# Low-rank time-step rows of a fused GNN, Mamba and mixture-of-experts kernel: plain fp32 in place of a split into reduced-precision parts

## The chip, the cores and the metric

The kernel runs on one core of one Trainium2 chip. The metric is device time in microseconds (us) of one launch; before the change the median of three runs is 1839.88 us (1839.81 to 1846.79).

## The reference, cut to what matters

`N` is 8192 rows of 128 features. A graph layer multiplies by a dense adjacency matrix of 8192 x 8192; its result goes through a Mamba block, and that through a layer with 8 experts.

```python
h = relu(adj @ layernorm(x) @ gcn_w + gcn_b); h = layernorm(h) * ln_g + ln_b
xz = h @ w_in;  xc, z = xz[:, :256], xz[:, 256:]
u = silu(conv4(xc) + conv_b)
dbc = u @ w_xp                                  # 8 + 16 + 16 columns
dt = softplus(dbc[:, :8] @ w_dt + b_dt)         # the eight low-rank rows of the time step
B, C = dbc[:, 8:24], dbc[:, 24:40]
# scan over the rows, 256 channels x 16 states: hst = exp(dt*A)*hst + dt*B*u;  y = hst @ C
x = x + ((y + u * D_skip) * silu(z)) @ w_out
H = gelu(layernorm(x) @ W1 + b1); probs = softmax(H @ Wg + bg)
out = x + probs[e] * (H @ Wd[e] + bd[e])        # e = argmax of probs, 512 hidden, 8 experts
```

The change touches `dbc[:, :8] @ w_dt` alone.

## The kernel before, in words

The 8192 rows are cut into 16 tiles of 512 (`T`). Tensors lie transposed, channels on the partitions and the 512 rows of a tile along the free axis. The kernel is a software pipeline written out by hand. Body `i` has five stages, each on another tile: `adjacency` for tile i+2, `front` (graph layer, projection, convolution, time step) for tile i+1, `mamba` (the scan) for tile i, `ffn` for tile i-1 and `experts` for tile i-2. A body has 16 slots (`SLOTS`), one for each Mamba state; slot `s` of each stage is written beside slot `s` of the others. Bodies 4 to 13 lie in a hardware loop of two bodies a round, the rest is unrolled. No scheduler orders anything: each engine runs its own instructions in the order written, and waits on semaphores.

What the engines do in a slot of a full body:

- VectorE (DVE): two scans (L609), the sums of the expert outputs that were read from PSUM (`combine`, L590 to L598), `y_sum` plus the last slot's `h_c` (L661), and `inject` for the next slot (L725).
- GpSimd (POOL): `h_c` = `hidden` times C (L355), which waits until `inject` of the next slot is done and so runs beside the scans. In four slots it also subtracts to form the low part of `H` (L346).
- TensorE (PE): four adjacency products of 128x512 (L781), and in every second slot one unit of twelve expert products into `ps_e` (`unit`); DVE's `combine(v)` reads unit v // 2.
- ScalarE (ACT): copies of the scan's last column (L406), the decays (L413), activations and copies out of PSUM.
- SyncE (SP): the DMAs, in order: adjacency blocks, each behind the matmuls that free its ring buffer (`adj_used`), and between them the broadcast rows of B and C (`bc_ring`), which go through DRAM (`bc_dram`).

The time step is made in slots 8 to 13 of `front`. In slot 8 PE multiplies `u_sb` by `w_xp`. The host has laid out `w_xp` so that the product holds B and C on partitions 96 to 127 and the same eight low-rank rows three times, from partitions 0, 32 and 64. In slot 9 ACT copies B and C (L495), casts partitions 0 to 71 to the reduced type fp32r into `low_parts` (L497), and copies the third set once more, uncast, into `low_raw` (L498). POOL then replaces rows 64 to 71 of `low_parts` by `low_raw` minus their cast (L339), after its `h_c` of slot 8 and ahead of that of slot 9. The weights `wdt_parts` hold, on partitions 0, 32 and 64, the cast, what the cast lost, and the cast, formed once at the start (ACT L388, DVE L565). One product of 72 partitions thus adds up high x high, high x rest and rest x high. PE makes it for the first 128 channels in slot 9 (it waits for `low_split`, POOL's semaphore) and for the other 128 in slot 10. DVE reads both in slot 11 (L632) and 13 (L637). Every product of the kernel that is in fp32r appears in the trace as one matmul, every plain fp32 product of 512 columns as two.

Behind the product of slot 10 PE has 16 gate products of 8 columns (for `logit`), six adjacency products, and unit 6, which DVE's `combine(12)` reads in slot 13. PE also waits for DVE: in slot 3 for `x1` (L622), in slot 14 for `coef_parts` (L712).

Of the kernel before, what the change touches and what calls it, by code (L numbers as in the profile page):

```python
# [5 lines left out]
P = 128  # L6
T = 512
SLOTS = 16
# [8 lines left out]
ALU = mybir.AluOpType  # L17
ACT = mybir.ActivationFunctionType
F32 = mybir.dt.float32
# [15 lines left out]
def gnn_mamba_moe(nc, x_rows, x_cols, adj, vecs, consts, sel, gcn_w, w_in, w_xp, w_dt, w_out, W1, Wg, Wd, bd, out):  # L35
# [10 lines left out]
    with ExitStack() as ctx:  # L46
# [19 lines left out]
        wdt_parts = sb("wdt_parts", [72, 2, P], F32R)  # L66
# [20 lines left out]
        low_parts = sb("low_parts", [96, T], F32R)  # L87
        coef_t = low_parts[:, 0:P]

        rows_sb = sb("rows_sb", [72, T])  # L90
        bc_rows, low_raw = rows_sb[0:2 * SLOTS, :], rows_sb[64:72, :]
# [31 lines left out]
        wdt_sb = x1[0:72, 0:2 * P].rearrange("p (h c) -> p h c", h=2)  # L123
# [69 lines left out]
        low_split = sem("low_split")  # L193
# [76 lines left out]
        def _(sp):  # L270
# [6 lines left out]
            def small_weights():  # L277
                for dst, src in ((vec_sb, vecs), (const_sb, consts), (gcn_sb, gcn_w), (win_sb, w_in),
                                 (wxp_sb, w_xp), (wdt_sb, w_dt), (wout_sb, w_out), (w1_sb, W1), (wg_sb, Wg),
                                 (bd_sb, bd)):  # L280
                    sp.dma_start(dst if isinstance(dst, bass.AP) else dst[:], src).then_inc(weights_in, 16)
# [46 lines left out]
        def _(pool):  # L328
            def body(i, p, adjacency, front, mamba, ffn, experts):
                c = Count(pool, i)  # L330
                q = 1 - p
                for s in range(SLOTS):

                    if front and s == 9:

                        if mamba:
                            c.wait(hc_ready, 0, s)
                        c.wait(low_ready, 1, 1)
                        nc.gpsimd.tensor_tensor(low_parts[64:72], low_raw, low_parts[64:72].bitcast(F32),  # L339
                                                ALU.subtract).then_inc(low_split, 1)  # L340
                        c.wait(low_split, 1, 1)
# [19 lines left out]
        def _(act):  # L361
# [26 lines left out]
            nc.scalar.copy(wdt_parts[:], wdt_sb)  # L388
# [8 lines left out]
            def body(i, p, adjacency, front, mamba, ffn, experts):  # L397
# [19 lines left out]
                for s in range(SLOTS):  # L417
# [73 lines left out]
                    if front and s == 9:  # L491

                        c.wait(dbc_done, 1, 1)
                        c.wait(rows_out, 1, 0)
                        nc.scalar.copy(bc_rows, ps_f[96:128, 0]).then_inc(rows_ready, 1)  # L495
                        c.wait(dt_done, 1, 0)
                        nc.scalar.copy(low_parts[0:72], ps_f[0:72, 0])  # L497
                        nc.scalar.copy(low_raw, ps_f[64:72, 0]).then_inc(low_ready, 1)  # L498
# [32 lines left out]
        def _(dve):  # L531
# [10 lines left out]
            for e in range(10):  # L542
# [11 lines left out]
                if e >= 2:  # L554
# [10 lines left out]
            nc.vector.tensor_tensor(wdt_parts[32:40], wdt_sb[32:40], wdt_parts[32:40].bitcast(F32), ALU.subtract  # L565
                                    ).then_inc(start_v, 1)
# [6 lines left out]
            dve.wait_ge(start_v, 9)  # L573
# [157 lines left out]
        def _(pe):  # L731
# [12 lines left out]
            def body(i, p, adjacency, front, mamba, ffn, experts):  # L744
                c = Count(pe, i)
                q = 1 - p
                for s in range(SLOTS):
# [37 lines left out]
                    if front and s == 0:  # L785
                        if isinstance(i, int) and i == -1:
                            pe.wait_ge(start_a, 3)
                            pe.wait_ge(start_v, 9)
                        c.wait(agg_ready, 1, 1)
                        c.wait(dt_ready, 1, 0)  # L790
                        product(ps_f[:, 0], [(gcn_sb[:], front_a[:])]).then_inc(gcn_done, 1)
# [35 lines left out]
                    if front and s == 9:  # L827
                        c.wait(low_split, 1, 1)
                        if ffn:
                            c.wait(h_ready, -1, 2)  # L830
                        product(ps_f[:, 1], [(wdt_parts[:, 0], low_parts[0:72])]).then_inc(dt_done, 1)
# [3 lines left out]
                    if front and s == 10:  # L835
                        c.wait(rows_ready, 1, 1)
                        product(ps_f[:, 0], [(wdt_parts[:, 1], low_parts[0:72])]).then_inc(dt_done, 1)
# [84 lines left out]
```

## Time and profile before

| | |
|---|---|
| median of three runs | 1839.88 us |
| the profiled execution | 1840.22 us |
| its span, from the first to the last instruction | 1838.1 us |
| PE busy | 1648.3 us (90%) |
| VectorE busy | 1663.1 us (90%) |
| ScalarE busy | 829.9 us (45%) |
| GpSimd busy | 708.7 us (39%) |
| POOL L339, the subtraction of the low rows | 16 of 1480 ns, 23.7 us |
| ACT L497, L498, the cast and the raw copy | 16 of 583 ns and 16 of 578 ns |
| PE products of `low_parts` with `wdt_parts` | 32, 642 ns in the record |

The 1.5 to 2 us between span and execution lie outside the instructions. A matmul's recorded duration contains its way through the array and overlaps the next one; what it costs the engine is the distance between starts. Idle time is shown in square brackets in a timeline, with what ended it. Two engines are about equally busy on average, so where the time goes has to be read from who waits for whom, stretch by stretch.

### The profile page before, as it was taken

The numbers are of one execution on the slowest core, as the hardware profiler recorded it, in microseconds if no ns is written. First come the engines' busy times: TensorE is split into PE (matmuls) and PEld (weight loads), VectorE is DVE, ScalarE is ACT, GpSimd is POOL, SyncE is SP. The second block draws the span as 40 slices with busy tenths as digits, with TensorE's granted clock in tenths as the row PEclk, the third lists the DMA queues.
The fourth block names the chain that finished last, engine by engine and source line by source line (L and its number), as shares of the span: only waits on it lengthen the run. The fifth ranks groups of instructions, "written<-read, shape, count | busy, mean of one in ns | idle before, by whom it ended". The sixth has DMA issues, their size and how long they took to land. (4 is left out here: it accounts for less than half of the span.)

```text
span 1838.1 us, 18846 instructions
## 1 busy us (share of the span) xinstructions
PE 1648.3 (90%) x4856; PEld 896.8 (49%) x4856; DVE 1663.1 (90%) x2089; ACT 829.9 (45%) x1457; POOL 708.7 (39%) x340
## 2 busy tenths in 40 slices
PE   5999697999999999999999999999999999764668
PEld 2444243555554555455554545455555555432447
DVE  8118999999999999999989999999999999999974
ACT  3034455463636354463625454363635446362522
POOL 0003444434444344434434444444434443444431
PEclk9999898999999999999999999999999999876779
DMA  9889786766677777667676776667776676322210
GB/s 334 289 258 354 279 292 251 252 238 254 240 271 248 258 246 250 231 219 280 236 258 223 266 252 238 233 221 284 247 250 241 241 256 229 116 88 86 100 33 12
DMA packets 124749, 420.56 MB, mean 229 GB/s; under 512 B 13404, under 2 KB 22180, under 8 KB 124420
## 3 DMA queue, kind: packets, MB, share of 16 engines
q1 hardware_dynamic: 123236, 413.51, 64.1%
q10 hardware_dynamic: 1440, 6.29, 0.9%
q14 instruction: 54, 0.44, 0.1%
q8 instruction: 19, 0.31, 0.1%
HBM read 414.51 MB, written 5.24 MB: 228 GB/s over the span
## 5 line engine op out<-in xcount | busy, mean ns | idle before, releaser
L781 PE MATMUL ps_adj<-ring,nodes 128*128 128x512 f32 x2048 | 962.9, 611 | 31.4 <-DVE nodes L557 17.4
L355 POOL TENSOR_TENSOR h_c<-hidden,bc_ring 128x1024 f32<-128x1024 f32 x256 | 605.0, 2363 | 946.4 <-DVE inject L725 865.4
L609 DVE TENSOR_TENSOR_SCAN hidden<-decay,state,inject 128x512 f32<-128x512 f32 x512 | 627.6, 1268 | 37.2 <-POOL h_c L355 9.3
L781 PEld LDWEIGHTS ps_adj<-ring,nodes 128*128 128x128 f32 x2048 | 397.7, 196 | 490.9 <-issue 449.0
L734 PE MATMUL ps_e<-wd_parts,H_parts 128*128 128x512 f32 x1536 | 437.6, 436 | 9.8 <-DVE odd_acc L593 5.3
L734 PEld LDWEIGHTS ps_e<-wd_parts,H_parts 128*128 128x128 f32 x1536 | 299.5, 196 | 129.2 <-issue 52.5
L413 ACT ACTIVATE decay<-dt_sb,negA 128x512 f32<-128x512 f32 x512 | 340.1, 713 | 1.3 <-DVE dt_sb L637 1.0
L725 DVE TENSOR_TENSOR inject<-dtu_sb,bc_ring 128x1024 f32<-128x1024 f32 x256 | 318.2, 1243 | 15.4 <-DMA bc_ring<-bc_dram 13.2
L661 DVE TENSOR_TENSOR y_sum<-y_sum,h_c 128x1024 f32<-128x1024 f32 x224 | 301.2, 1345 | 0.5 <-POOL h_c L355 0.4
L406 ACT COPY state<-hidden 128x2 f32<-128x2 f32 x256 | 49.4, 193 | 515.5 <-DVE hidden L609 515.1
L593 DVE SCALAR_TENSOR_TENSOR out_sb<-ps_e,coef,out_sb 128x128 f32<-128x128 f32 x256 | 84.7, 331 | 31.1 <-PE ps_e L734 28.8
L346 POOL TENSOR_TENSOR H_parts<-H,H_parts 128x512 fp32r<-128x512 f32 x64 | 82.3, 1286 | 38.5 <-ACT H_parts L518 38.5
L674 DVE SCALAR_TENSOR_TENSOR u_sb<-conv_in,vec_sb,u_sb 128x512 f32<-128x512 f32 x96 | 65.0, 746 | 11.3 <-ACT u_sb L466 11.3
L339 POOL TENSOR_TENSOR low_parts<-rows_sb,low_parts 8x512 fp32r<-8x512 f32 x16 | 23.7, 1480 | 125.1 <-ACT rows_sb L498 123.4
L734 PEld LDWEIGHTS ps_y<-wg_sb,H 128*128 128x128 f32 x512 | 65.5, 207 | 9.8 <-ACT H L525 6.0
L734 PE MATMUL ps_y<-wg_sb,H 128*128 128x8 f32 x512 | 64.1, 265 | 5.5 <-ACT H L525 5.5
L593 DVE SCALAR_TENSOR_TENSOR odd_acc<-ps_e,coef,odd_acc 128x128 f32<-128x128 f32 x192 | 65.7, 342 | 0.0
L734 PE MATMUL ps_y<-x,const_sb 128*128 128x512 f32 x32 | 21.5, 759 | 46.2 <-DVE x L622 46.2
L734 PE MATMUL ps_f<-front_a,win_sb 128*128 128x512 f32 x128 | 60.3, 594 | 1.3 <-ACT conv_in L459 1.2
L625 DVE TENSOR_TENSOR front_a<-ps_f,front_b 128x512 f32<-128x512 f32 x16 | 10.8, 677 | 42.8 <-ACT front_b L440 42.8
L734 PE MATMUL ps_f<-soft,w_sb 128*128 128x512 f32 x64 | 33.8, 655 | 15.0 <-DVE soft L665 15.0
L734 PE MATMUL ps_f<-u_sb,wxp_sb 128*128 128x512 f32 x64 | 35.5, 683 | 13.0 <-ACT H L487 8.3
(108 smaller groups left out, 1100.7 us busy)
## 6 DMA issues: line engine op xcount, KB each, us to landing
ring<-adj SPq DMA_DIRECT2D x512, 512.0 KB, 4.2
bc_ring<-bc_dram SPq DMA_DIRECT2D x256, 512.0 KB, 4.8
nodes<-x_rows ACTq DMA_DIRECT2D x8, 512.0 KB, 12.4
x_tile<-x_cols SPq DMA_DIRECT2D x16, 256.0 KB, 5.7
out<-out_sb SPq DMA_DIRECT2D x16, 256.0 KB, 4.0
decay<-Wd ACTq DMA_DIRECT2D x1, 1024.0 KB
dt_sb<-Wd ACTq DMA_DIRECT2D x1, 1024.0 KB
bc_dram<-rows_sb SPq DMA_DIRECT2D x16, 64.0 KB
```

The lines of the kernel that those rows point to most:

```text
L339: nc.gpsimd.tensor_tensor(low_parts[64:72], low_raw, low_parts[64:72].bitcast(F32), ALU.subtract).then_inc(low_split, 1)
L346: nc.gpsimd.tensor_tensor(H_parts[:, 1, place], H[:, :, b * P:(b + 1) * P], H_parts[:, 0, place].bitcast(F32), ALU.subtract).then_inc(lo_s ...
L355: nc.gpsimd.tensor_tensor(h_c[:, s % 2], hidden[:, s % 2], over_halves(bc_ring[:, s % BC_RING, 1]), ALU.mult).then_inc(hc_ready, 1)
L406: nc.scalar.copy(state[:, :, t:t + 1], hidden[:, t % 2, :, T - 1:T]).then_inc(state_ready, 1)
L413: exp = nc.scalar.activation(decay[:, t % 2, h], dt_sb[:, p if d == 0 else q, h], ACT.Exp, scale=negA[:, h, t:t + 1])
L593: step = nc.vector.scalar_tensor_tensor(out=acc, in0=src, scalar=w, in1=acc, op0=ALU.mult, op1=ALU.add)
L609: scan = nc.vector.tensor_tensor_scan(hidden[:, s % 2, h], decay[:, s % 2, h], inject[:, h], state[:, h, s:s + 1], ALU.mult, ALU.add)
L661: nc.vector.tensor_tensor(y_sum[:], y_sum[:], h_c[:, (s - 1) % 2], ALU.add).then_inc(y_step, 1)
L674: nc.vector.scalar_tensor_tensor(out=u_sb[:, h], in0=conv_in[:, h, k:k + T], scalar=vec("conv_w", TAPS * h + k), in1=u_sb[:, h], op0=ALU.m ...
L725: nc.vector.tensor_tensor(inject[:], dtu_sb[:], over_halves(bc_ring[:, t % BC_RING, 0]), ALU.mult).then_inc(inject_ready, 1)
L734: last = nc.tensor.matmul(dst, stationary, moving, start=(n == 0), stop=(n == len(pairs) - 1))
L781: last = nc.tensor.matmul(ps_adj[:, 0], nodes[:, m], ring[:, g % RING, m % GROUP], start=(m == 0), stop=(m == J - 1))
```

## The change

The eight rows are copied once out of PSUM as plain fp32 (`low_sb`), and the weights are the eight rows as loaded. The cast, the raw copy, POOL's subtraction with its semaphore, and the two set-up instructions for the weights go. Both products are plain fp32 over 8 partitions. Buffers that shared memory with these (`coef_t`, `bc_rows`) get their own.

```diff
-        wdt_parts = sb("wdt_parts", [72, 2, P], F32R)
+        wdt_sb = sb("wdt_sb", [8, 2, P])
...
-                    if front and s == 9:
-
-                        if mamba:
-                            c.wait(hc_ready, 0, s)
-                        c.wait(low_ready, 1, 1)
-                        nc.gpsimd.tensor_tensor(low_parts[64:72], low_raw, low_parts[64:72].bitcast(F32),
-                                                ALU.subtract).then_inc(low_split, 1)
-                        c.wait(low_split, 1, 1)
...
-            nc.scalar.copy(wdt_parts[:], wdt_sb)
...
                         c.wait(dt_done, 1, 0)
-                        nc.scalar.copy(low_parts[0:72], ps_f[0:72, 0])
-                        nc.scalar.copy(low_raw, ps_f[64:72, 0]).then_inc(low_ready, 1)
+                        nc.scalar.copy(low_sb[:], ps_f[0:8, 0]).then_inc(low_ready, 1)
...
-            nc.vector.tensor_tensor(wdt_parts[32:40], wdt_sb[32:40], wdt_parts[32:40].bitcast(F32), ALU.subtract
-                                    ).then_inc(start_v, 1)
...
                     if front and s == 9:
-                        c.wait(low_split, 1, 1)
+                        c.wait(low_ready, 1, 1)
                         if ffn:
                             c.wait(h_ready, -1, 2)
-                        product(ps_f[:, 1], [(wdt_parts[:, 0], low_parts[0:72])]).then_inc(dt_done, 1)
+                        product(ps_f[:, 1], [(wdt_sb[:, 0], low_sb[:])]).then_inc(dt_done, 1)
...
                     if front and s == 10:
                         c.wait(rows_ready, 1, 1)
-                        product(ps_f[:, 0], [(wdt_parts[:, 1], low_parts[0:72])]).then_inc(dt_done, 1)
+                        product(ps_f[:, 0], [(wdt_sb[:, 1], low_sb[:])]).then_inc(dt_done, 1)
```

PE's instructions in slots 9 and 10 of a full body, before (`soft` holds the normalized input of the expert layer, `w_sb` is W1, `[waits ...]` names the semaphores):

```order
L734 MATMUL ps_f<-low_parts,wdt_parts 128x512 [waits h_ready,low_split]
L734 MATMUL ps_y<-soft,w_sb 128x512 [waits h_ready]
L781 MATMUL ps_adj<-ring,nodes 128x512 [waits ring_in0]
L781 MATMUL ps_adj<-ring,nodes 128x512
L734 MATMUL ps_e<-wd_parts,H_parts 128x512 [waits acc_step]
L734 MATMUL ps_e<-wd_parts,H_parts 128x512 x11
L781 MATMUL ps_adj<-ring,nodes 128x512 [waits ring_in1]
L781 MATMUL ps_adj<-ring,nodes 128x512
L734 MATMUL ps_f<-low_parts,wdt_parts 128x512 [waits rows_ready]
```

The same place after the change:

```order
L719 MATMUL ps_f<-low_sb,wdt_sb 128x512 [waits h_ready,low_ready]
L719 MATMUL ps_y<-soft,w_sb 128x512 [waits h_ready]
L766 MATMUL ps_adj<-ring,nodes 128x512 [waits ring_in0]
L766 MATMUL ps_adj<-ring,nodes 128x512
L719 MATMUL ps_e<-wd_parts,H_parts 128x512 [waits acc_step]
L719 MATMUL ps_e<-wd_parts,H_parts 128x512 x11
L766 MATMUL ps_adj<-ring,nodes 128x512 [waits ring_in1]
L766 MATMUL ps_adj<-ring,nodes 128x512
L719 MATMUL ps_f<-low_sb,wdt_sb 128x512 [waits rows_ready]
```

Nothing has moved; the first product waits for ACT's semaphore where it waited for POOL's, and the operands are others.

POOL's instructions around slot 9, before (the first `h_c` is that of slot 8):

```order
L355 TENSOR_TENSOR h_c<-hidden,bc_ring 128x1024 [waits y_step,inject_ready]
L224 REGISTER_ALU [waits hc_ready]
L339 TENSOR_TENSOR low_parts<-rows_sb,low_parts 8x512 [waits low_ready]
L224 REGISTER_ALU [waits scan_ready,low_split]
L355 TENSOR_TENSOR h_c<-hidden,bc_ring 128x1024 [waits y_step,inject_ready]
```

The same place after the change:

```order
L344 TENSOR_TENSOR h_c<-hidden,bc_ring 128x1024 [waits y_step,inject_ready]
L221 REGISTER_ALU [waits scan_ready]
L344 TENSOR_TENSOR h_c<-hidden,bc_ring 128x1024 [waits y_step,inject_ready]
L221 REGISTER_ALU [waits scan_ready]
L344 TENSOR_TENSOR h_c<-hidden,bc_ring 128x1024 [waits y_step,inject_ready]
```

POOL goes from one `h_c` to the next, and its wait for its own subtraction is gone too.

## Rows read from the trace of the kernel before

**Rows 1.** Busy time by engine in the last stretch (start:end, length, busy)

```profile
1771.00:1838.00 67.00, 60.88 (x251) 46.45 (x251) 30.63 (x90) 14.34 (x21) 9.41 (x8) 0.93 0.04 12
```

**Rows 2.** Waits of DVE, 400 to 1600 us: waiter, awaited: total us, times, longest

```profile
DVE hidden L609 <- POOL h_c L355: 9.3, 3, 3.3
...
DVE out_sb L593 <- PE ps_e L734: 1.2, 1, 1.2
```

**Rows 3.** Waits of PE, 400 to 1600 us

```profile
PE ps_y L734 <- DVE x L622: 29.1, 9, 8.9
...
PE ps_f L734 <- POOL low_parts L339: 10.5, 10, 1.4
```

**Rows 4.** Timeline of slot 9 in one full body: start, length, what

```profile
901.05 3.60 PE L781 MATMUL ps_adj<-ring,nodes 128*128 128x512 f32 x8
...
902.52 0.58 ACT L498 COPY rows_sb<-ps_f 8x512 f32<-8x512 f32 x1
...
904.35 1.26 POOL L339 TENSOR_TENSOR low_parts<-rows_sb,low_parts 8x512 fp32r<-8x512 f32 x1 [0.16 <-DVE hidden L609]
...
904.71 1.98 DVE L661 TENSOR_TENSOR y_sum<-y_sum,h_c 128x1024 f32<-128x1024 f32 x1
...
905.74 0.49 PE L734 MATMUL ps_f<-low_parts,wdt_parts 72*128 72x512 f32 x1 [1.09 <-POOL low_parts L339]
...
906.07 1.02 PE L734 MATMUL ps_y<-soft,w_sb 128*128 128x512 f32 x2
```

**Rows 5.** All of L661 and of L725: ns minimum/median/maximum

```profile
L661 DVE TENSOR_TENSOR y_sum<-y_sum,h_c x224: 1207/1217/2295, 157.4 to 1771.4; 128x1024 f32<-128x1024 f32 x112
...
L725 DVE TENSOR_TENSOR inject<-dtu_sb,bc_ring x256: 1218/1226/2301, 144.6 to 1765.2; 128x1024 f32<-128x1024 f32 x128
```

**Rows 6.** Slot 9 of two other bodies, timeline of DVE and PE

```profile
801.33 2.27 DVE L661 TENSOR_TENSOR y_sum<-y_sum,h_c 128x1024 f32<-128x1024 f32 x1
...
802.65 0.49 PE L734 MATMUL ps_f<-low_parts,wdt_parts 72*128 72x512 f32 x1
...
1636.51 1.94 DVE L661 TENSOR_TENSOR y_sum<-y_sum,h_c 128x1024 f32<-128x1024 f32 x1
```

**Rows 7.** Timeline of PE around the second product, slot 10

```profile
911.45 1.88 PE L781 MATMUL ps_adj<-ring,nodes 128*128 128x512 f32 x4
...
912.76 0.79 PE L734 MATMUL ps_f<-low_parts,wdt_parts 72*128 72x512 f32 x1
...
913.40 4.72 PE L734 MATMUL ps_y<-wg_sb,H 128*128 128x8 f32 x32
```

**Rows 8.** Unit 6 on PE and its first reader on DVE, in four bodies

```profile
822.01 3.36 PE L734 MATMUL ps_e<-wd_parts,H_parts 128*128 128x512 f32 x12
...
825.50 0.35 DVE L593 SCALAR_TENSOR_TENSOR out_sb<-ps_e,coef,out_sb 128x128 f32<-128x128 f32 x1
...
925.06 3.35 PE L734 MATMUL ps_e<-wd_parts,H_parts 128*128 128x512 f32 x12
...
928.54 0.35 DVE L593 SCALAR_TENSOR_TENSOR out_sb<-ps_e,coef,out_sb 128x128 f32<-128x128 f32 x1
...
1031.69 3.36 PE L734 MATMUL ps_e<-wd_parts,H_parts 128*128 128x512 f32 x12
...
1035.61 0.33 DVE L593 SCALAR_TENSOR_TENSOR out_sb<-ps_e,coef,out_sb 128x128 f32<-128x128 f32 x1
...
1245.71 0.35 DVE L593 SCALAR_TENSOR_TENSOR out_sb<-ps_e,coef,out_sb 128x128 f32<-128x128 f32 x1 [1.16 <-PE ps_e L734]
```

**Rows 9.** Timeline of PE, SP and DVE at the start of the first scan

```profile
126.58 15.61 PE L781 MATMUL ps_adj<-ring,nodes 128*128 128x512 f32 x36
...
137.45 0.42 SPq L309 DMA_DIRECT2D bc_ring<-bc_dram  x1
...
144.59 1.23 DVE L725 TENSOR_TENSOR inject<-dtu_sb,bc_ring 128x1024 f32<-128x1024 f32 x1 [13.18 <-DMA bc_ring<-bc_dram]
```

**Rows 10.** Busy by stretch; the third figure from the end is TensorE's granted clock

```profile
915.00:920.00 5.00, 5.00 (x22) 3.97 (x22) 4.91 (x8) 3.29 (x7) 0.71 (x2) 0.57 0.46 185
```

More of the change, by code:

```diff
@@ L85, in gnn_mamba_moe @@
         dtu_sb = sb("dtu_sb", [P, 2, T])
[L87 to L91, printed above, removed]
+        coef_t = sb("coef_t", [96, P], F32R)[:]
+        low_sb = sb("low_sb", [8, T])
+        bc_rows = sb("bc_rows", [2 * SLOTS, T])[:]
         bc_ring = sb("bc_ring", [P, BC_RING, 2, T])
@@ L122, in gnn_mamba_moe @@
         bd_sb = soft[0:96, 1].rearrange("p (b c) -> p b c", b=BLOCKS)
-        wdt_sb = x1[0:72, 0:2 * P].rearrange("p (h c) -> p h c", h=2)
         row_sum, row_rstd = odd_acc[:, 0:J], odd_acc[:, J:2 * J]
@@ L192, in gnn_mamba_moe @@
         base_done, base_ready = sem("base_done"), sem("base_ready")
-        low_split = sem("low_split")
         hi_split, lo_split = sem("hi_split", BLOCKS), sem("lo_split", BLOCKS)
@@ L278, in small_weights @@
                 for dst, src in ((vec_sb, vecs), (const_sb, consts), (gcn_sb, gcn_w), (win_sb, w_in),
-                                 (wxp_sb, w_xp), (wdt_sb, w_dt), (wout_sb, w_out), (w1_sb, W1), (wg_sb, Wg),
+                                 (wxp_sb, w_xp), (wdt_sb, w_dt[0:8]), (wout_sb, w_out), (w1_sb, W1), (wg_sb, Wg),
                                  (bd_sb, bd)):
@@ L572, in _ @@
                                         ).then_inc(start_v, 1)
-            dve.wait_ge(start_v, 9)
+            dve.wait_ge(start_v, 8)
             def body(i, p, adjacency, front, mamba, ffn, experts):
@@ L787, in body @@
                             pe.wait_ge(start_a, 3)
-                            pe.wait_ge(start_v, 9)
+                            pe.wait_ge(start_v, 8)
                         c.wait(agg_ready, 1, 1)
```

## The prediction

> **What bounds the kernel now.** I read the busy shares first. PE and DVE both stand at 90%, so the shares decide nothing. Next the waits of each engine in the steady part, 400 to 1600 us. DVE waits there for others 9.3 us at three scans behind POOL, 1.2 us once for PE, and some 8 us in pieces that I leave aside [rows 2]: under 20 of 1200 us. PE waits 29.1 us for DVE's x1 and 10.5 us for the subtraction of the low rows, in ten bodies [rows 3], and more for other results of DVE. So DVE sets the length of a body, and PE follows with a few us of slack in each. The last stretch is PE's: 60.9 us busy of 67, against 30.6 for DVE [rows 1]; the time step is not made there, and it begins when DVE releases it. What counts is therefore what DVE gains in each body, and whether PE, which gets more work, can follow.
>
> **DVE's gain.** DVE has no instruction less in a body. But POOL's subtraction collides with it. In rows 4 POOL runs from 904.35 to 905.61, and DVE's y_sum, started at 904.71 inside that time, takes 1.98 us; the median of all y_sum is 1.22 us [rows 5]. Its end lies 1.08 us behind POOL's end, nearly a whole undisturbed y_sum: it waited until POOL was through, then ran. When the subtraction begins a little behind y_sum, the next instruction, inject, pays: 2.30 us instead of 1.23 [rows 5]. I went through all sixteen subtractions. The first has no DVE work beside it. Of the other fifteen, eleven stretch a y_sum, by 0.72 to 1.06 us (2.27 at 801.33, 1.98 at 904.71, 1.94 at 1636.51, the last) [rows 4, 6], together 22.55 minus 11 x 1.22 = 9.1 us; four stretch an inject, 4 x 1.07 = 4.3 us [rows 5]. Sum 13.4 us, all in stretches in which DVE goes from one instruction to the next. With the subtraction gone nothing of POOL stands at this place, since its next `h_c` waits for inject. Bounds: 0 if the cause were another, 13.4 if the whole is given back. I take the whole, because both forms of the collision leave the same signature.
>
> The Trainium skill (SBUF — State Buffer, section "Who interferes with whom") says that a DVE instruction with two SBUF inputs and a GpSimd instruction that reads SBUF exclude each other, and that the later one waits for the whole of the other. By that rule y_sum in rows 4 should pay what was left of POOL's 1.26 us, 0.90; the trace shows 0.76 more than the median, so nearly that.
>
> **ACT.** One copy of 0.58 us goes in each body. The first copy, which alone remains, ended before 902.52, when the raw copy began [rows 4]; ACT is busy 45% of the time. I cost this at nothing: ACT's next work, the decays, are awaited by DVE nowhere in rows 2. For PE the operand is ready at 902.5 instead of 905.6.
>
> **PE's cost.** A plain fp32 product of 512 columns is two records, whose starts lie 0.43 us apart ((3.60 - 0.59) / 7 for the eight of rows 4), so 0.86 us. The fp32r product: its four predecessors begin at 911.45 and use up four turns of 0.43 to 913.17; the next product begins at 913.40 [rows 7]. So it cost 0.23 us, and plain fp32 costs 0.63 more. No row shows a product over 8 partitions. Bounds: 0.43 us (if half the passes sufficed) to 0.86 for the product; I take 0.86, since the fp32r product over 72 partitions is priced like a full one. Two products a body: +1.25 us, 20 us over 16 tiles.
>
> The Trainium skill (FP8 and Floating Point Precision, "TensorE Precision Notes") gives true fp32 four passes through the array. With the fp32r product as one pass that would be 4 x 0.23 = 0.92 us, an estimate from that page, and 1.4 us a body instead of 1.25; this rule speaks against the change.
>
> **PE's gain.** In slot 9 PE is through at 901.05 + 8 x 0.43 = 904.48 and waits for POOL until 905.74; the next product begins at 906.07 [rows 4]. After the change the low product begins at 904.48 and its successor at 905.34: 0.73 us earlier. The second product takes back 0.63. Net, PE arrives 0.10 us earlier behind slot 10. In bodies where PE comes later there is no wait to save: at 802.65 it went straight from an adjacency product into the low product [rows 6], and the whole 1.25 us is added.
>
> **Where the two meet.** The nearest reader is unit 6: DVE wants it in slot 13. The slack there (DVE's start minus PE's recorded end) is 0.13 us at 825.50 and at 928.54, 0.56 at 1035.61, and at 1245.71 DVE already waits 1.16 us (0.12 remaining) [rows 8]. In the eight other bodies in which all five stages are alive it is 1.66 to 3.45 us, and at every other unit 3.4 us or more. DVE comes there earlier by its gain, PE by its own. What DVE loses again:
> - body of 825.50: gain 1.05 (2.27 - 1.22), PE later by 1.25, slack 0.12: 1.05 + 1.25 - 0.12 = 2.2 us
> - body of 928.54: 0.76 - 0.10 - 0.13 = 0.5 us
> - body of 1035.61: gain 1.07; PE waited 0.93 (its gap in starts), so it is later by 0.2; slack 0.56: 0.7 us
> - body of 1245.71: gain 1.07, PE waited 0.92, slack 0.12: 1.2 us
> - the others: at most 1.07 + 0.2 against 1.66: nothing
>
> Sum 4.6 us. This tightness is partly the clock's: behind the gate products PE's granted clock was 0.57 of full on average between 915 and 920 [rows 10], which means 1.2 instead of 2.4 GHz for part of it, and how often that falls there differs from body to body. So the 4.6 us may become 1 or 9.
>
> **The start.** Before the first scan DVE waits 13.18 us for a load of bc_ring. SP issues it at 137.45, behind adjacency loads that wait for PE's matmuls, and PE works without a gap from 126.58 [rows 9]. The first low product there saves no wait (PE had adjacency work until then), so +1.25 us. The set-up loses two instructions of 0.4 us beside the adjacency stream of the first tile, worth nothing.
>
> **Sum.** -13.4 + 4.6 + 1.25 = -7.5 us. On the profiled execution of 1840.2 us that is 1832.7; the median of the runs lies 0.3 lower, so I say **1832.5 us**.
>
> **The rivals.**
> A. *All of it is given back.* PE idles less for POOL, its clock stays high more often, and unit 6 is nowhere late. For it: eight of twelve bodies have the slack, and the clock dips move with the shorter body. Against it: four bodies lie at the edge. 1839.9 - 13.4 + 1.25 = 1827.7 us.
> B. *PE becomes the second bound and eats the gain.* In most bodies the dip of the clock falls behind the gate products in full, the slack is 0.1 as at 825.50, and DVE loses about the 0.8 us that it gained. Then only the four tiles outside the steady part keep their gain: three with 1.07, 1.07 and 0.72, and the first, which costs 1.25. About -2 us: 1838 us. It is also what comes out if the collisions are hidden for a reason that I do not see.
> C. *Slower.* PE comes late in every steady body, as at 802.65, where it had no wait for POOL: each of the twelve then costs 1.25 - 0.1 instead of gaining, 13.8 us, plus 1.25 at the start, minus the 2.9 us outside: 1852 us. It decides where PE's slack at unit 6 is below what PE adds. For it: two products at nearly four times the price on an engine 90% busy. Against it: PE had to wait for POOL in ten bodies of the steady part and 29 us for x1 [rows 3], so it is not late as a rule.
>
> **How the numbers follow.** Forecast 0.45, A 0.25, B 0.20, C 0.10. Below 0.5% (9.2 us) a measurement of this kernel can't tell a change from none, so faster means under 1830.7: A and a sixth of the forecast, 0.33. Slower means over 1849.1: half of C, 0.05. The rest, 0.62, is no change. The range runs from 1826.5 (A, with some luck of the clock) to 1841 (past B) and leaves out most of C; the bounds of the product over 8 partitions (down to 0.43 us, which frees PE by 0.9 us a body and leads to A) lie within it.
>
> **What would show it.** No y_sum or inject beside slot 9 over 1.3 us. The low product's records as two, 0.43 us apart, and PE's next start 0.86 us behind; no wait of PE for POOL in slot 9. DVE's waits for `ps_e` up from 1.2 us to some 6 us in the steady part, in slot 13. The first inject about 1.25 us later. I am wrong if DVE's y_sum still stretches there, if the distance behind the low product is not 0.86 us, or if DVE waits for PE at other places than unit 6.

## The result, and the profile after

The change made the kernel slower by half a per cent, where I had forecast a gain of 0.4%.

| | median, us | lowest to highest | runs |
|---|---|---|---|
| before | 1839.86 | 1838.03 to 1846.79 | 16 |
| changed | 1849.66 | 1844.57 to 1863.60 | 16 |

The ratio of changed to before is 1.0055, with a 95% interval of 1.0037 to 1.0074. The changed kernel also scatters more, over 19 us instead of 9. The mean granted clock of TensorE over the run goes with it, roughly: 0.932 in the two of 1863 us, 0.937 to 0.943 in the three shortest. The profiled execution is one of the two longest (1863.28 us, span 1861.4), so its trace shows the effect larger than the median does.

Below, **half-clock time** is the time in a trace during which the granted clock was 1.2 instead of 2.4 GHz. Where no trace is at hand it is worked out from an execution's span and mean granted clock, as 2 x (1 - clock) x span; which comes out some 2 us under a trace's own sum. By that estimate the changed kernel has 229 us (median of its 16 executions), and the kernel before 206 (106 executions beside the experiments).

What went as predicted comes first. DVE's collisions with the subtraction in slot 9 are gone. These are all y_sum and all inject of the changed kernel (ns minimum/median/maximum):

```profile
L646 DVE TENSOR_TENSOR y_sum<-y_sum,h_c x224: 1207/1218/2287, 161.8 to 1795.8; 128x1024 f32<-128x1024 f32 x112
...
L710 DVE TENSOR_TENSOR inject<-dtu_sb,bc_ring x256: 1218/1227/1235, 148.6 to 1789.5; 128x1024 f32<-128x1024 f32 x128
```

No inject is over 1.24 us, where four had taken 2.30 [rows 5]; all 27 y_sum over 1.5 us that are left run beside POOL's subtraction for `H`. Over the whole span y_sum and inject are busy 290.2 + 314.0 = 604.2 us, against 301.2 + 318.2 = 619.4 before: 15.2 us less, where I had said 13.4. DVE's busy time as a whole fell by 12.0 us, from 1663.1 to 1651.1.

PE's slots 9 and 10, in the body whose like stands in rows 6:

```profile
804.62 2.74 PE L766 MATMUL ps_adj<-ring,nodes 128*128 128x512 f32 x6
807.29 1.12 PE L719 MATMUL ps_f<-low_sb,wdt_sb 8*128 8x512 f32 x2
808.34 1.13 PE L719 MATMUL ps_y<-soft,w_sb 128*128 128x512 f32 x2
...
813.82 1.88 PE L766 MATMUL ps_adj<-ring,nodes 128*128 128x512 f32 x4
815.62 1.12 PE L719 MATMUL ps_f<-low_sb,wdt_sb 8*128 8x512 f32 x2
816.67 5.72 PE L719 MATMUL ps_y<-wg_sb,H 128*128 128x8 f32 x32
822.25 8.42 PE L766 MATMUL ps_adj<-ring,nodes 128*128 128x512 f32 x12
830.11 2.19 PE L719 MATMUL ps_e<-wd_parts,H_parts 128*128 128x512 f32 x7
```

There is no wait for POOL. The low product of slot 10 holds PE for longer than my 0.86 us ("holds" is the time from when the record before it could have made way to the next instruction's start): the four adjacency records before it use their turns up to 813.82 + 4 x 0.43 = 815.54, and the gate products begin at 816.67, so 1.13 us. Then the gate products take 5.6 us (816.67 to 822.25) where 16 of them took 3.4 at full clock, and the twelve adjacency records behind them 7.9 us (to 830.11) where twelve at 0.43 are 5.2. Busy times by stretch show why (start:end, length, busy of PE, weight loads, DVE, ACT, POOL, then granted clock, DMA share, GB/s):

```profile
805.00:818.00 13.00, 13.00 (x44) 6.76 (x42) 12.82 (x18) 8.51 (x15) 4.88 (x3) 1.00 0.69 232
818.00:828.00 10.00, 10.00 (x29) 6.75 (x29) 9.71 (x14) 4.32 (x9) 4.05 (x2) 0.51 0.27 102
828.00:833.60 5.60, 5.60 (x19) 3.40 (x18) 0.77 (x2) 1.95 (x4) 0.65 (x1) 0.97 0.67 244
```

PE is busy without a break in all three, yet its clock is 1.2 instead of 2.4 GHz for the ten us from 818, beginning 1.4 us after the low product of slot 10 made way for the gate products (816.67). In the third row DVE is busy for 0.77 of 5.6 us. It waits for unit 6:

```profile
833.60 0.35 DVE L578 SCALAR_TENSOR_TENSOR out_sb<-ps_e,coef,out_sb 128x128 f32<-128x128 f32 x1 [4.83 <-PE ps_e L719]
```

The waits of DVE between 400 and 1600 us (total, times, longest), which answer to rows 2:

```profile
DVE out_sb L578 <- PE ps_e L719: 27.3, 9, 4.8
DVE hidden L594 <- issue: 12.5, 7, 5.5
DVE hidden L594 <- POOL h_c L344: 5.8, 2, 3.2
```

The wait for `ps_e` went from 1.2 us to 27.3, in nine of twelve bodies. Nothing else of this size is new: the two rows of `hidden` together are 18.3 us, where they were 13.4 (9.3 and 4.1). The half-clock time in the whole trace went from 208 to 253 us. The end of the program has not changed: from 1795 us PE is busy for 59.9 of 66.4 us as in rows 1. The last stretch was reached 24 us later.

So the question is why PE is late: through the clock, and if so, whether that belongs to the change or is a chance of timing.

### The profile page after: what moved, and what is told of

The parts are those of the page before. It is cut to its first block and busy times, and to the rows that moved or that the text cites. A ratio compares the mean times of both kernels' runs of the same rounds, so it can differ in the third digit from the quotient of the medians.

```text
span 1861.4 us, 18846 instructions
## 1 busy us (share of the span) xinstructions
PE 1699.4 (91%) x4888; PEld 917.8 (49%) x4888; DVE 1651.1 (89%) x2088; ACT 818.4 (44%) x1440; POOL 685.8 (37%) x324
## 5 line engine op out<-in xcount | busy, mean ns | idle before, releaser
L766 PE MATMUL ps_adj<-ring,nodes 128*128 128x512 f32 x2048 | 973.1, 617 | 32.9 <-DVE nodes L544 16.8
L710 DVE TENSOR_TENSOR inject<-dtu_sb,bc_ring 128x1024 f32<-128x1024 f32 x256 | 314.0, 1227 | 16.6 <-DMA bc_ring<-bc_dram 14.2
L646 DVE TENSOR_TENSOR y_sum<-y_sum,h_c 128x1024 f32<-128x1024 f32 x224 | 290.2, 1295 | 0.0
L719 PEld LDWEIGHTS ps_y<-wg_sb,H 128*128 128x128 f32 x512 | 78.6, 246 | 16.7 <-issue 10.6
L719 PE MATMUL ps_y<-wg_sb,H 128*128 128x8 f32 x512 | 80.0, 298 | 5.5 <-ACT H L512 5.5
L719 PE MATMUL ps_f<-soft,w_sb 128*128 128x512 f32 x64 | 33.9, 655 | 14.5 <-DVE soft L650 14.5
L505 ACT CAST H_parts<-H 128x512 fp32r<-128x512 f32 x64 | 39.3, 616 | 4.0 <-PE ps_e L719 4.0
```

The costliest lines, as they stand in the source:

```text
L505: nc.scalar.copy(H_parts[:, 0, split_buffer(parity, b)], H[:, :, b * P:(b + 1) * P]).then_inc(hi_split, 1)
L646: nc.vector.tensor_tensor(y_sum[:], y_sum[:], h_c[:, (s - 1) % 2], ALU.add).then_inc(y_step, 1)
L710: nc.vector.tensor_tensor(inject[:], dtu_sb[:], over_halves(bc_ring[:, t % BC_RING, 0]), ALU.mult).then_inc(inject_ready, 1)
L719: last = nc.tensor.matmul(dst, stationary, moving, start=(n == 0), stop=(n == len(pairs) - 1))
L766: last = nc.tensor.matmul(ps_adj[:, 0], nodes[:, m], ring[:, g % RING, m % GROUP], start=(m == 0), stop=(m == J - 1))
```

## The experiments

**My theory** after the result: the plain fp32 products fill only 8 of the array's 128 rows, and the clock falls earlier and for longer for it, close to the small gate products. **The rival**: PE's engine time is what counts, and the dips of the clock are a by-product of the timing. All ratios are to runs of the kernel before on the same chip (median 1840.1 to 1840.6 us). Where a trace's half-clock time or waits are given, they are those of one execution.

**128 rows instead of 8.** The weights are zero in rows 8 to 127, and ACT copies all 128 rows of the product in PSUM.

```diff
-        wdt_sb = sb("wdt_sb", [8, 2, P])
+        wdt_sb = sb("wdt_sb", [128, 2, P])
...
-        low_sb = sb("low_sb", [8, T])
+        low_sb = sb("low_sb", [128, T])
...
-                        nc.scalar.copy(low_sb[:], ps_f[0:8, 0]).then_inc(low_ready, 1)
+                        nc.scalar.copy(low_sb[:], ps_f[0:128, 0]).then_inc(low_ready, 1)
```

> The changed kernel, but the plain fp32 product runs over 128 partitions: ACT copies all of PSUM's 128 rows, and the weights are zero outside the first eight. The number of matmuls, their columns and all waits are those of the changed kernel. Clock theory (the two plain fp32 products that fill only 8 of the 128 rows count as little work, so together with the gate products behind them they bring TensorE's clock down earlier and for longer): the half-clock time falls from 253 us towards the 208 us of the kernel before, DVE waits for ps_e in the steady part for under 10 us instead of 27, time 1830 to 1840 us. Rival (only the engine time of the products counts, 1.25 us a body, wherever it comes from): nothing changes against the changed kernel, 1845 to 1855 us, half-clock time 240 us or more, DVE waits for ps_e above 20 us.

1834.52 us (1833.51 to 1840.18), ratio to before 0.9972, interval 0.9958 to 0.9987. It is 15 us faster than the changed kernel with the same number of matmuls, columns and waits. Half-clock time 202 us. Every range of the clock theory is met, none of the rival's. Its PE in the same place, and DVE's waits:

```profile
807.76 1.88 PE L766 MATMUL ps_adj<-ring,nodes 128*128 128x512 f32 x4
809.48 1.02 PE L719 MATMUL ps_f<-low_sb,wdt_sb 128*128 128x512 f32 x2
810.34 4.61 PE L719 MATMUL ps_y<-wg_sb,H 128*128 128x8 f32 x32
814.80 7.77 PE L766 MATMUL ps_adj<-ring,nodes 128*128 128x512 f32 x12
822.01 3.36 PE L719 MATMUL ps_e<-wd_parts,H_parts 128*128 128x512 f32 x12
```

```profile
DVE hidden L594 <- POOL h_c L344: 11.7, 4, 3.0
DVE out_sb L578 <- PE ps_e L719: 3.8, 6, 0.7
```

The low product takes 0.86 us from start to start, as worked out ahead, and from its start to that of unit 6 there are 12.5 us instead of 14.5. DVE waits 3.8 us for `ps_e` instead of 27.3. So the number of rows matters, with the same instructions and semaphore waits. But one thing is not alike: from 807.76 + 4 x 0.43 = 809.48 the low product here holds PE for 0.86 us, with 8 rows for 1.13. That is 0.28 us a product more, some 0.57 a body, at full clock. I saw it only later, and come back to it below.

**The gain without the price.** The kernel before, without POOL's subtraction. It leaves out the term rest x high of the low rows (their weights are zero), so it does not compute all that the reference asks:

```diff
-                        nc.gpsimd.tensor_tensor(low_parts[64:72], low_raw, low_parts[64:72].bitcast(F32),
-                                                ALU.subtract).then_inc(low_split, 1)
...
-                        nc.scalar.copy(low_parts[0:72], ps_f[0:72, 0])
-                        nc.scalar.copy(low_raw, ps_f[64:72, 0]).then_inc(low_ready, 1)
+                        nc.scalar.copy(low_parts[0:72], ps_f[0:72, 0]).then_inc(low_ready, 1)
```

> The kernel before with the subtraction on GpSimd and the raw copy taken away; the fp32r product over 72 partitions stays (left out: the term rest x high of the low rows, its weights are zero). It is the gain of the change without its price. Both theories: no y_sum or inject stretched in slot 9, 13 us of DVE time back, PE freed of 1.1 us of waiting a body, so PE is never late: 1825 to 1830 us. If the gain was mis-sized (the collisions were hidden by something else): 1836 us or more.

1828.66 us (1825.15 to 1831.31), ratio 0.9930 (0.9916 to 0.9944). The gain that I put down to the collisions exists; in time it is 12 us of the 13.4 here. What is missing may be the start, where the first dtu begins at 133.6 us instead of 130.2 in this kernel too (see below).

**The price without the gain.** The changed kernel with a subtraction on dummy data at the old place:

```diff
+                        c.wait(low_ready, 1, 1)
+                        nc.gpsimd.tensor_tensor(low_dummy[:], low_sb[:], low_sb[:],
+                                                ALU.subtract).then_inc(low_split, 1)
...
-                        c.wait(low_ready, 1, 1)
+                        c.wait(low_split, 1, 1)
```

> The changed kernel with GpSimd's subtraction put back on dummy data at the old place, PE's first low product waiting for it as before. It is the price of the change without its gain. Engine-time theory: each body's PE is later by 1.25 us than in the kernel before, DVE keeps its collisions, so unit 6 is late by up to 1.25 us less the slack in twelve bodies: 1845 to 1855 us. Clock theory: the clock falls as in the changed kernel, so DVE waits at unit 6 as long as there while paying 13 us for collisions: 1855 to 1865 us.

1861.18 us (1855.71 to 1863.31), ratio 1.0106 (1.0089 to 1.0122). Plain fp32 over 8 rows costs 21 us by itself; the range of the clock theory is met, that of engine time missed. But the range for engine time was worked out with 1.25 us a body, before I knew of the longer hold.

**The fourth corner.** The same with 128 rows, weights and copy alike; the subtraction reads rows 0 to 7:

```diff
-        low_sb = sb("low_sb", [8, T])
+        low_sb = sb("low_sb", [128, T])
```

> The fourth corner beside the changed kernel (8 rows, no subtraction, 1850 us), e1_rows128 (128 rows, none, 1834.5) and e3_pool_kept (8 rows, subtraction kept, 1861): plain fp32 over 128 rows with the subtraction kept. If the fill of the rows and the subtraction cost separately, it is 1861 - 15 = 1846 us, and what it stands above the kernel before, 6 us, is the pure engine time of plain fp32. If the fill only helps where the subtraction is gone: 1855 us or more.

1845.02 us (1841.04 to 1849.91), ratio 1.0025 (1.0013 to 1.0037), against 1846 us expected if fill and subtraction cost separately. With it the four medians make a table whose differences nearly add up:

| us | 8 rows | 128 rows | filling the rows brings |
|---|---|---|---|
| subtraction kept | 1861.2 | 1845.0 | 16.2 |
| subtraction gone | 1849.7 | 1834.5 | 15.2 |
| taking it away brings | 11.5 | 10.5 | |

From the kernel before, 1840: the subtraction gone, -11; the engine time of plain fp32, +5 (1845.0 against 1840.1); eight rows instead of 128, +15 to 16, whatever it is about them. Sum 1849 to 1850, the changed kernel.

**Which of the two products?** Only the one in slot 10, or only the one in slot 9, over 128 rows. Each edit is against the 128-row kernel and takes one product back to 8 rows, first that of slot 9:

```diff
-                        product(ps_f[:, 1], [(wdt_sb[:, 0], low_sb[:])]).then_inc(dt_done, 1)
+                        product(ps_f[:, 1], [(wdt_sb[0:8, 0], low_sb[0:8])]).then_inc(dt_done, 1)
```

> As e1_rows128, but only the product of slot 10, which stands right ahead of the gate products, runs over 128 partitions; that of slot 9 has 8. If what matters is the one stretch of product and gate products in slot 10, this one alone gives back nearly all: 1834 to 1839 us. If each product of 8 rows costs its share wherever it stands: half way between 1834.5 and 1849.7, so 1840 to 1845 us.

1838.20 us (1835.34 to 1842.90), ratio 0.9986 (0.9975 to 0.9997). Then that of slot 10:

```diff
-                        product(ps_f[:, 0], [(wdt_sb[:, 1], low_sb[:])]).then_inc(dt_done, 1)
+                        product(ps_f[:, 0], [(wdt_sb[0:8, 1], low_sb[0:8])]).then_inc(dt_done, 1)
```

> The counterpart: the product of slot 9 over 128 partitions, that of slot 10 over 8. By the first theory of e5_second128 little is given back: 1845 to 1852 us; by the second 1840 to 1845 us.

1853.64 us (1843.81 to 1858.28), ratio 1.0055 (1.0034 to 1.0077). Eight rows in slot 9 cost 4 us; in slot 10, right ahead of the gate products, 19 by the medians and 15 by the ratios (the second has only six executions, and they lie far apart). The first time is within the range of "one stretch in slot 10", the second above both ranges. Half-clock time is 209.5 us in the first and 253.7 in the second, as in the changed kernel.

**The gate products in two halves.**

```diff
-                        for b in range(BLOCKS):
+                        for b in range(2):
                             last = product(ps_y[:, 0, b * EXPERTS:(b + 1) * EXPERTS],
                                            [(H[:, k, b * P:(b + 1) * P], wg_sb[:, k]) for k in range(4)])
+                    if ffn and s == 11:
+                        for b in range(2, BLOCKS):
...
```

> The changed kernel with the 16 gate products cut in two: those of two row blocks in slot 10, those of the other two in slot 11, so that four adjacency products lie between the two halves. PE has the same work in all. Clock theory: no stretch with little work is left, the clock stays at 2.4 GHz behind slot 10 in most bodies, unit 6 is ready in time: 1825 to 1832 us, half-clock time under 200 us. Engine-time theory: PE's amount of work is unchanged, 1845 us or more.

1842.10 us (1837.88 to 1845.40), ratio 1.0005 (0.9995 to 1.0015). It lies between the ranges of the two theories and meets neither; only its half-clock time, under 200 us, is as the clock theory had it. 7.6 us came back, with the 8-row products and their engine time in place. It fell to 198 us, and DVE waits 1.1 us for `ps_e`. But the logits come one slot later, and DVE waits for those:

```profile
DVE hidden L594 <- POOL h_c L344: 9.2, 3, 3.3
DVE logit L666 <- PE ps_y L719: 6.5, 4, 2.6
```

**An attempt at a better version**: 128 rows, and the low product of slot 10 between two halves of the gate products.

```diff
-                    if front and s == 10:
+                    if front and not ffn and s == 10:
...
                         for b in range(BLOCKS):
+                            if front and b == BLOCKS // 2:
+                                c.wait(rows_ready, 1, 1)
+                                product(ps_f[:, 0], [(wdt_sb[:, 1], low_sb[:])]).then_inc(dt_done, 1)
```

> A version meant to be better than both: e1_rows128, and in slot 10 PE makes the gate products of two row blocks, then the low product over 128 partitions, then the gate products of the other two, so that the stretch of small products is cut in two without delaying the logits. Clock theory: the half-clock time behind slot 10 falls below that of e1_rows128 (202 us in all), DVE's remaining waits at unit 6 (3.8 us) go: 1828 to 1833 us. If 1.7 us of small products are as bad as 3.4, it is as e1_rows128, 1834 us.

1839.56 us (1833.11 to 1847.63), ratio 0.9988 (0.9970 to 1.0005): a miss. The half-clock time rose to 215 us (one of the longer executions), and DVE waits 5.1 us for the delayed low product in slot 11.

**The disputed cost by itself.** At the very end of the 128-row kernel PE makes 128 more products, whose results are not used:

```diff
             bodies(pe, body)
+            for n in (8, 32, 64, 128):
+                for k in range(32):
+                    product(ps_f[:, 0], [(wdt_sb[0:n, 0], low_sb[0:n])])
```

> The disputed cost by itself: e1_rows128, and at the very end PE makes 32 plain fp32 products of 512 columns back to back over 8 partitions, then 32 each over 32, 64 and 128 (their results are not used). Clock theory: PE is busy without a gap, and yet its granted clock falls to half during the products over 8 partitions (0.86 us between the starts of two records, 1.7 us a product) and is full during those over 128 (0.43 us). Rival (the rows do not matter to the clock): full clock in all four streams, 32 x 0.86 = 27.5 us each.

Busy time by stretch, columns as above; each stretch lies inside one stream:

```profile
1832.00:1883.00 51.00, 51.00 (x64) 19.89 (x63) 0.94 (x4) 0.00 (x0) 0.00 (x0) 0.52 0.02 5
1884.00:1937.00 53.00, 53.00 (x64) 20.58 (x62) 0.00 (x0) 0.00 (x0) 0.00 (x0) 0.50 0.00 0
1938.00:1992.00 54.00, 54.00 (x65) 21.08 (x64) 0.00 (x0) 0.00 (x0) 0.00 (x0) 0.50 0.00 0
1998.00:2022.00 24.00, 24.00 (x57) 10.64 (x56) 0.00 (x0) 0.00 (x0) 0.00 (x0) 1.00 0.00 0
```

PE is busy without any gap, and yet its clock is 1.2 GHz through the streams over 8 (from 3 us after its start), 32 and 64 rows; over 128 it rises to 2.4. So the clock theory is met as far as it goes, but 32 and 64 rows began at a clock that was already low. The same with other numbers, `for n in (64, 72, 96, 8)`:

> As e8_stream, with the streams over 64, 72, 96 and again 8 rows. If anything above 64 rows counts as filled: half clock in the first, full in the second and third, half in the last. If the clock wants nearly all rows: half clock in all four. In all cases the last stream shows that order does not decide.

```profile
1834.00:1860.00 26.00, 26.00 (x62) 11.30 (x61) 0.65 (x3) 0.00 (x0) 0.00 (x0) 1.00 0.04 10
1861.00:1887.00 26.00, 26.00 (x62) 11.53 (x61) 0.00 (x0) 0.00 (x0) 0.00 (x0) 1.00 0.00 1
1889.00:1915.00 26.00, 26.00 (x62) 11.60 (x61) 0.00 (x0) 0.00 (x0) 0.00 (x0) 1.00 0.00 0
1921.00:1967.00 46.00, 46.00 (x55) 17.89 (x54) 0.00 (x0) 0.00 (x0) 0.00 (x0) 0.50 0.00 0
```

Neither of my two expectations for this second trace fits, and the level at the start does count. 64 rows keep 2.4 GHz here, where the stream began at it, and in the first trace did not regain it, where it began at 1.2. Eight rows bring the clock down from full in both. The Trainium skill (TensorE: Matmul & The Clock Gate, "Why this matters for your kernels") says that a single product with a contraction of 32 takes as long as one of 128. By that rule all streams last the same. The trace agrees at equal clock, 64 rows and 128 both at 0.43 us a record; so do the first records over 8 rows, at 0.43. But as soon as the clock has fallen, 3 us into that stream, a record over 8 rows takes 0.85: the time is the same only while the clock is.

**64 rows in the kernel**, and **72** (`[72, T]`), weights and copy alike:

```diff
-        low_sb = sb("low_sb", [8, T])
+        low_sb = sb("low_sb", [64, T])
```

> The changed kernel with 64 rows. In e8_stream the products over 64 rows ran at half clock like those over 8, and only those over 128 at full clock. If that holds in the kernel: like the changed kernel, 1845 to 1855 us. If the clock asks for the share of filled rows in proportion: half way to e1_rows128, 1840 to 1843 us.

1845.96 us (1836.92 to 1854.57), ratio 1.0033 (1.0015 to 1.0052), in the range expected if 64 rows are like 8.

> The changed kernel with 72 rows. The product's hold of PE should be the short one, 0.86 us from start to next start, since the 72-row fp32r products of the kernel before had their loads issued ahead. If the clock too counts anything above 64 rows as filled: 1833 to 1836 us, as e1_rows128. If it counts 72 of 128 as little work: 1840 to 1847 us.

1838.41 us (1832.84 to 1844.62), ratio 0.9993 (0.9982 to 1.0004), between the two expected ranges. The hold of PE steps between the two. Slot 10 with 64 rows, then with 72:

```profile
812.31 1.12 PE L719 MATMUL ps_f<-low_sb,wdt_sb 64*128 64x512 f32 x2
813.37 5.50 PE L719 MATMUL ps_y<-wg_sb,H 128*128 128x8 f32 x32
...
806.37 1.02 PE L719 MATMUL ps_f<-low_sb,wdt_sb 72*128 72x512 f32 x2
807.23 4.58 PE L719 MATMUL ps_y<-wg_sb,H 128*128 128x8 f32 x32
```

The next instruction begins 1.05 us behind the start of the 64-row product, as with 8, and 0.86 behind the 72-row one. The weight loads (PEld) show where the time goes. In slot 10 with 64 rows, then with 72:

```profile
812.31 0.29 PEld L719 LDWEIGHTS ps_f<-low_sb,wdt_sb 64*128 64x128 f32 x2 [0.76 <-issue]
...
805.94 0.19 PEld L719 LDWEIGHTS ps_f<-low_sb,wdt_sb 72*128 72x128 f32 x1 [0.24 <-issue]
806.37 0.19 PEld L719 LDWEIGHTS ps_f<-low_sb,wdt_sb 72*128 72x128 f32 x1 [0.24 <-issue]
```

Over 72 rows the load begins a whole record (0.43 us) ahead of its product. Over 64 it begins with the product, 0.1 us after the record before could have made way, and that of the successor likewise; 8 rows are as 64, 128 as 72. The loss belongs to the change of rows, not to the short product as such: inside the streams above the records over 64 rows follow each other at 0.43 us, but the first over 72 begins 0.52 us behind the last over 64, and the first over 96 again 0.43 behind the last over 72.

The time with 64 rows is above that with 128 (ratios 1.0033 and 0.9972, intervals apart). With 72 it is 4 us above by the medians, though PE is held no longer and DVE waits 3.8 us for `ps_e` in both; the intervals overlap a little, and that difference stays open.

**Time or clock?** So 8 rows differ from 128 in two things, and my first experiment had changed both. Here the rows are full, and PE is held as long as with 8 rows, by one more product over 170 columns:

```diff
+                        product(ps_f[:, 1, 0:170], [(wdt_sb[:, 0], low_sb[:, 0:170])])
                         product(ps_f[:, 1], [(wdt_sb[:, 0], low_sb[:])]).then_inc(dt_done, 1)
...
+                        product(ps_f[:, 0, 0:170], [(wdt_sb[:, 1], low_sb[:, 0:170])])
                         product(ps_f[:, 0], [(wdt_sb[:, 1], low_sb[:])]).then_inc(dt_done, 1)
```

> e1_rows128, and ahead of each low product one more over 128 rows and 170 columns into the same bank, overwritten by the real one: 2 x 0.14 us of PE more a product, 0.57 us a body, as much as the 8-row products hold PE longer, but with full rows. If the clock is what the 8 rows cost: 1834.5 plus little, 1836 to 1839 us. If the longer hold of PE is what costs: as the changed kernel, 1847 to 1852 us.

1847.68 us (1844.60 to 1848.92), ratio 1.0036 (1.0023 to 1.0049), in the range for "the longer hold costs". In slot 10 the hold is 1.14 us, as wanted:

```profile
811.18 1.31 PE L719 MATMUL ps_f<-low_sb,wdt_sb 128*128 128x170 f32 x4
812.32 4.45 PE L719 MATMUL ps_y<-wg_sb,H 128*128 128x8 f32 x32
```

My theory in its pure form falls: 0.57 us a body, 9 us over 16 tiles, cost 13, with full rows and 209 us at half clock. DVE waits 13.8 us for `ps_e`. The 64-row kernel, with the same hold, has nearly the same: 1846.0 us, 14.2 us of waits. And in one slot only, slot 10 and slot 9:

> e1_rows128 with the added product over 170 columns in slot 10 only: PE's times are those of e6_first128 (8 rows in slot 10), its rows are full. If the few rows of slot 10 bring the clock down beyond what the time does: clearly under the 1853.6 us of e6_first128, 1837 to 1843 us, half-clock time near 205 us where e6 had 254. If only PE's time matters: 1848 us or more.

1837.29 us (1829.96 to 1842.12), ratio 0.9980 (0.9965 to 0.9994), half-clock time 184 us: in time as expected if the few rows bring the clock down.

> The same with the added product in slot 9 only: PE's times are those of e5_second128 (8 rows in slot 9), its rows are full. e5 was 1838.2 us. Both theories: 1836 to 1841 us. If it is 1845 us or more, an added time in either slot is amplified and my reading of e5 is wrong.

1838.42 us (1833.58 to 1845.29), ratio 0.9990 (0.9975 to 1.0006), 186 us, in the range of both theories.

| PE held 0.28 us longer in | by 8 rows | by a full product |
|---|---|---|
| slot 9 | 1838.2 | 1838.4 |
| slot 10 | 1853.6 | 1837.3 |
| both | 1849.7 | 1847.7 |

In slot 9 only the time counts. In slot 10 the same time costs 3 us with full rows and 19 (15 by the ratios) with eight: there the rows bring the clock down. The traces have 254 us at half clock with eight rows and 184 with full ones, but the first is of that kernel's longest execution. The medians over all executions, worked out from span and clock as above, say the same with less:

| kernel | half-clock time, us | executions |
|---|---|---|
| before | 206 | 106 |
| changed | 229 | 16 |
| 8 rows, subtraction kept | 230 | 6 |
| 8 rows in slot 10 only | 235 | 6 |
| 8 rows in slot 9 only | 196 | 12 |
| 64 rows | 210 | 9 |
| 72 rows | 204 | 12 |
| 128 rows | 198 | 7 |
| 128 rows, subtraction kept | 201 | 12 |
| full product added in both slots | 207 | 5 |
| full product added in slot 10, in slot 9 | 195, 200 | 11, 12 |

Only the three kernels with 8 rows ahead of the gate products stand out, by their medians; single executions overlap less or more (changed 210 to 253, 64 rows 198 to 222, full product in both slots 195 to 210). 64 rows hold PE as long as 8 and do not stand out.

In both slots the time alone is already worth 13 us, and the rows add 2, which their intervals (1.0023 to 1.0049 and 1.0037 to 1.0074) do not tell apart. So both causes are shown, the rows' in time only where slot 10 alone has eight, and they do not add. I read it as either one using up the slack at unit 6; no run shows that by itself. That the changed kernel is not slower than the one with 8 rows in slot 10 alone is within the noise of the second: both have the ratio 1.0055.

**The kernel before with 128 rows.** Slot 9; slot 10, the weights and the copy alike:

```diff
-                        product(ps_f[:, 1], [(wdt_parts[:, 0], low_parts[0:72])]).then_inc(dt_done, 1)
+                        product(ps_f[:, 1], [(wdt_parts[:, 0], low_parts[:])]).then_inc(dt_done, 1)
```

> The kernel before with its two fp32r products a body over 128 partitions instead of 72 (zero weights in the added rows). Its products are short, 0.23 us, so by the clock theory little can be won: 1836 to 1840 us, half-clock time at or a little under 208 us. 1832 us or less would mean that the kernel before too loses much to them.

1838.66 us (1837.73 to 1845.45), ratio 0.9994 (0.9984 to 1.0003), half-clock time 209.5 us. No difference that can be told, as expected: its products over 72 rows were on the cheap side already.

## Why the prediction was wrong, step by step

- **What bounds the kernel**: right. DVE sets the length of a body, and PE has a few us of slack, least at unit 6.
- **DVE's gain**: right. 15.2 us less of busy y_sum and inject, against 13.4 worked out; 10.5 to 11.5 us in time in the table of four.
- **PE's cost: this step failed.** I wrote that no row shows a product over 8 partitions, bounded it by 0.43 to 0.86 us, and took 0.86 "since the fp32r product over 72 partitions is priced like a full one". It is 1.13 to 1.15 us, above my upper bound: a product over 8 rows (or 64, the other number tried) between products over 128 does not get its load ahead, nor lets the next. 0.57 us a body more, with full rows, cost 13 us. And it has a second price behind it, the clock, which I had not tied to it at all: 229 us at half clock against 207 with full rows held as long; in time 2 us that can't be told from none in the changed kernel, and 14 to 16 where slot 10 alone has eight rows. 72 is on the other side of that step, so the row that I drew on could not show either.
- **PE's gain**: the wait for POOL went, as said, but net PE is 0.47 us later behind slot 10, by this reckoning, not 0.10 us earlier: 2 x 0.28 us more.
- **Where the two meet**: the place was right, the size not. I put some 5 us there and said that the clock might make it 1 or 9; in the profiled execution, one of the two longest, it was 27.3. With full rows it is 3.8 us, and plain fp32 over full rows with the subtraction kept costs +5 us against the kernel before, near the 4.6 + 1.25 of the sum. What I missed here: added time costs more than its own size once PE is late. 0.28 us a body (4.6 us over 16 tiles) cost 3 or 4 us, 0.57 (9 us) cost 13.
- **The start**: not settled. The first dtu begins at 133.6 us instead of 130.2 and the first inject at 148.6 instead of 144.6, where I had said +1.25 for the latter. But the kernel with only the subtraction taken away has 133.6 too, and others lie between 131 and 135.5, without an order that PE's time would explain.
- **The rivals**: C, at 0.10, named what happened, PE late at unit 6 in most steady bodies (nine of twelve), though not its causes.
- **The sum**: it put the change at 1832.5 us, and the 128-row kernel, in which the product costs what I had taken, is near it: 1834.5. The longer hold adds 13 us and the 8 rows another 2: 1849.7.
- Of the 23 us between the two traces some 3 are a longer stop of DVE at the turn of the hardware loop (16.1 us in four turns, 13.4 before, 11.7 in the 128-row kernel). What lengthens it I can't say.

Of the versions that compute the whole reference the 128-row one has the lowest median, 1834.5 us: the change, with 120 rows of zero weights.

## What to carry to other kernels

When a product has a short contraction and stands among full ones, try filling the array's rows with zero weights where that is free: here it turned +0.55% into -0.28%. Before an instruction of an engine near the bound is exchanged, count its slack at the tightest reader, and take no price from a row of another shape across a step in size: bound it upward too. An experiment that changes one number may change two things; look in its trace for the second before the first is believed.

## What the runs showed of the hardware

- TensorE can be granted 1.2 GHz while it is busy without a gap (0.50 of full over the 53 us from 1884): products over 8 rows brought the clock down within 3 us of their start in both streams. Over 64 rows it stayed at the level that it had (0.50 in one stream, 1.00 in the other); over 128 it rose.
- The rows added to the eight had zero weights, and that was enough: 229 us at half clock became 198.
- Among full products a plain fp32 product over 8 or 64 rows held PE for 1.13 to 1.15 us, one over 72 or 128 for 0.86. The difference arises where a product over 8 or 64 rows meets one over 72 or more: 0.52 instead of 0.43 us from the last record over 64 rows to the first over 72.
